# Attention on one Trainium2 core: ScalarE builds ten of sixteen mask rows, and TensorE's loop over the head pairs is written out

## What is computed

```python
seq = (x @ W_seq).reshape(N, H, DH)                 # N 2048, H 16, DH 32
scores = score1[:, :, None] + score2[:, None, :]    # s1 of row i plus s2 of column j, per head
scores = jax.nn.leaky_relu(scores, negative_slope=0.2)
scores = scores + (1.0 - adj)[None, :, :] * MASK_VAL
attn = jax.nn.softmax(scores, axis=-1)
hidden = jnp.einsum('hij,jhd->ihd', attn, seq).reshape(N, D_IN)
```

## Time and profile before

| What | Value |
|---|---|
| median of the runs | 1131.07 us |
| the profiled execution | 1135.76 us, its span 1133.9 us |
| first matmul of the attention | at 123.15 us |
| last reduction of the attention starts | at 562.38 us |
| mean granted TensorE clock | 0.964 |

### The profile page before, as it was taken

The page is one execution under the profiler, slowest core; times in us unless marked ns, Lnnn a source line. Parts: engine busy times, 40 slices in busy tenths (PEclk is TensorE's granted clock), DMA queues, the critical chain, the costliest instruction groups (busy, mean ns, idle before and its releaser), DMA issues. The chain is left out here.

```text
span 1133.9 us, 27344 instructions
## 1 busy us (share of the span) xinstructions
PE 1042.5 (92%) x11304; PEld 916.3 (81%) x11304; DVE 856.1 (75%) x1216; ACT 618.2 (55%) x939; POOL 315.0 (28%) x287
## 2 busy tenths in 40 slices
PE   5799687989898989978899999999999999999998
PEld 4576587989898989978867788888888887777887
DVE  4756999999999999997359953345876558985554
ACT  2226777777777777773045543334445445664432
POOL 1101434444444445463234200000026300005510
PEclk9899898999898989898989999999999999999999
DMA  8356011111111111153073510002016213444242
GB/s 299 112 192 240 20 58 40 40 40 40 40 46 52 40 40 40 40 168 113 2 285 123 174 58 1 1 1 75 1 48 212 85 42 126 131 130 150 75 141 101
DMA packets 51472, 102.68 MB, mean 91 GB/s; under 512 B 5889, under 2 KB 25985, under 8 KB 48770
## 3 DMA queue, kind: packets, MB, share of 16 engines
q1 hardware_dynamic: 44386, 81.68, 21.2%
q10 hardware_dynamic: 3888, 10.72, 2.6%
q0 software_dynamic: 3072, 8.39, 2.3%
HBM read 74.69 MB, written 26.08 MB: 89 GB/s over the span
## 5 line engine op out<-in xcount | busy, mean ns | idle before, releaser
L791 PE MATMUL bank<-arena 128*128 128x132 f16 x4096 | 298.0, 226 | 52.6 <-issue 43.3
L600 ACT ACTIVATE arena<-arena 128x1024 fp8e4<-128x1024 f32 x288 | 303.2, 1135 | 7.4 <-DMA arena<-s_rows 4.5
L791 PEld LDWEIGHTS bank<-arena 128*128 128x128 fp8e4 x4096 | 256.1, 100 | 56.8 <-issue 56.8
L653 DVE TENSOR_SCALAR arena<-arena 128x1024 uint8<-128x1024 f32 x224 | 205.9, 988 | 0.0
L1170 PE MATMUL bank<-xt,up_parts 128*128 128x512 f32 x768 | 186.3, 391 | 0.0
L1637 PE MATMUL bank<-down_parts,h_parts 128*128 128x512 f32 x768 | 184.5, 389 | 0.1
L795 PE MATMUL bank<-arena 128*128 128x66 f16 x4096 | 179.3, 199 | 0.0
L1637 PEld LDWEIGHTS bank<-down_parts,h_parts 128*128 128x128 f32 x768 | 144.0, 188 | 30.5 <-issue 0.5
L1170 PEld LDWEIGHTS bank<-xt,up_parts 128*128 128x128 f32 x768 | 142.3, 188 | 28.7 <-ACT relu_sb L1119 0.2
L795 PEld LDWEIGHTS bank<-arena 128*128 128x128 fp8e4 x4096 | 160.8, 100 | 0.0
L1144 DVE TENSOR_TENSOR relu_sb<-relu_sb 128x512 f32<-128x512 f32 x64 | 44.3, 692 | 116.9 <-ACT relu_sb L1119 111.7
(11 more groups left out here) (225 smaller groups left out, 1477.8 us busy)
## 6 DMA issues: line engine op xcount, KB each, us to landing
hid<-in_adjT SPq DMA_DIRECT2D x16, 1024.0 KB, 4.9
arena<-s_rows SPq DMA_DIRECT2D x30, 512.0 KB, 3.8
sorted_latent_rows<-zeros SPq DMA_DIRECT2D x1, 4992.0 KB, 18.7
xs<-sorted_latent_rows SPq DMA_DIRECT2D x39, 128.0 KB, 2.2
sorted_expert_rows<-expert_y SPq DMA_DIRECT2D x39, 128.0 KB, 1.7
arena<-in_x SPq DMA_DIRECT2D x4, 1024.0 KB, 12.0
xr<-in_x SPq DMA_DIRECT2D x16, 256.0 KB, 2.8
up_sb<-in_upT ACTq DMA_DIRECT2D x1, 4096.0 KB, 14.7
```

Source lines behind the costliest of these rows:

```text
L600: last = nc.scalar.activation(m8[:, k, j, :], s1b[:, k % 2, :], ACT.Sigmoid, bias=bias_now[:, k // 2, j:j + 1], scale=STEEP, saturate=False)
L653: last = nc.vector.tensor_scalar(mu8[:, k, j, :], s1b[:, k % 2, :], neg_s2[:, 2 * p + k // 2, j:j + 1], float(ONE8), ALU.is_gt, ALU.mult)
L791: last = nc.tensor.matmul(o, m8[:, k, j, i * P:(i + 1) * P], vs[:, b, j, :], start=(j == 0), stop=(j == T - 1))
```

## The change

VectorE's share of the rows goes from seven to six and ScalarE's from nine to ten. The hardware loop of TensorE becomes a Python loop: the same eight pairs of four units stand one behind the other in the program, with constant semaphore values. A semaphore increment (`pe_passed`), for which nobody waits, goes away. The other engines keep their loops.

```diff
-DVE_J = 7
+DVE_J = 6
...
-        act_passed, pe_passed = sem("act_passed"), sem("pe_passed")
+        act_passed = sem("act_passed")
...
-                with pe.Fori(0, PAIRS) as p:
+                for p in range(PAIRS):
                     for k in range(4):
                         b = k // 2
                         if k % 2 == 0:
                             pe.wait_ge(lo_ready, 2 * p + b + 1)
                         pe.wait_ge(sums_ready, 4 * p + k + 1)
                         pe.wait_ge(m_ready, 4 * p + k + 1)
-                        pe.sem_inc(pe_passed, 1)
                         for i in range(IT):
```

## The result

The changed kernel takes 1088.01 us (median of 4 runs, 1087.89 to 1089.21), the kernel before beside it 1132.41 us (4 runs). The ratio is 0.9615, with a 95% interval of 0.9595 to 0.9634. The forecast was 1086 us, in a range of 1078 to 1104. Of the two profiled executions, 1135.76 us became 1088.03, 47.7 us less.

A forecast was written before the change was run, and what follows sets the result against it. VectorE and TensorE were taken as both at their limit in the attention loop. 36.0 us up to the twenty-eighth collect and 9.1 behind it, together 45.1, took the median 1131.07 to 1086 us, range 1078 to 1104.

The forecast's parts named there:

- Two limits at once: Attention loop: VectorE (53.6 us per four units) and TensorE (52.9) both at their limit; one edit alone gains almost nothing.
- VectorE's two units, 24.24 us: VectorE's period in the loop after the change: 20.94 undisturbed, less 1.35 for compares, plus 4.65 disturbance.
- The masks cancelled: VectorE's L661 and L668: 256 words move from one mask to the other, 0.27 us each way, nothing in sum.
- The disturbance: Time VectorE loses to GpSimd per two units: taken as 4.65 us, with ends 4.65 and 5.84.
- the cheaper order of L661 and L737: Shared ports: VectorE's L661 stands ahead of GpSimd's L737 in every pair; if not, 1102 us, chance 0.20.
- The reading beside the fill: TensorE fetching straight code while the zero fill holds the DMA engines: 0 to 6 us, taken as 1.
- Its cover: ScalarE's wait of 5.81 us for the build absorbs its extra rows; about 1.2 us stays, cost 0.
- The ring that the slower rival supposed: ScalarE's wait before L608 is no slack but part of a cycle; 28.2 us per two units, 1141 us, chance 0.05.
- The start: Before the loop: VectorE's fewer compares and mask words bring the first collect 2.3 us sooner, to 153.1.
- The sum: Whole kernel: 36.0 us sooner at the twenty-eighth collect and 9.1 behind it, together 45.1 us.
- The clock rival: TensorE's clock falls at the remaining waits, one fall of 2.79 us per two units; 1107 us, chance 0.07.

The follow-up runs named there:

- rows_only: Kernel before with only the rows moved (VectorE six, ScalarE ten), TensorE's hardware loop kept: 1126.1 us, ratio 0.9921.
- unroll_only: Changed kernel with VectorE back at seven rows, so only TensorE's loop is written out: 1128.32 us, ratio 0.9965 to the kernel before.
- rows_7_6: Changed kernel with VectorE making seven rows in even units, six in odd ones: 1118.21 us, ratio 0.9870 to the kernel before.
- rows_6_7: Changed kernel with VectorE making six rows in even units, seven in odd ones: 1096.61 us, ratio 0.9679 to the kernel before.
- rows_6_5: Changed kernel with VectorE making six rows in even units, five in odd ones: 1079.04 us, ratio 0.9522 to the kernel before.
- fill_later: Kernel before with SyncE's zero fill issued after unit 28, behind the last jump of TensorE's loop: 1128.72 us, ratio 0.9963.
- half_jumps: Kernel before with VectorE at six rows and TensorE's loop as four passes of eight units, three jumps back: 1095.47 us, ratio 0.9672.
- rows_5: Changed kernel with VectorE at five rows and ScalarE at eleven in all units: 1088.24 us, ratio 0.9605 to the kernel before.

## Why the prediction was right

**Two limits at once.** This was the main step, and rows_only and unroll_only bear it out: 0.8% and 0.35% alone, 3.85% together.

**VectorE's two units, 24.24 us.** Measured 24.07. The row gave its 0.67 (six undisturbed compares take 4.06 us, seven 4.72). The masks cancelled: 1.76 and 2.82 us undisturbed, in sum as before. The disturbance was put at 4.65 and is 24.07 - 19.59 = 4.48. That the cheaper order of L661 and L737 becomes the regular one was argued from one pair of units before, and only two of that trace had it; it held in every pair, and rows_7_6 against rows_6_7 shows what the other order costs, 1.4 us per two units. The prediction named a rule of the Trainium skill in SBUF — State Buffer, section Who interferes with whom: whoever issues first holds the shared ports, and the other one blocks. The traces agree with both halves. In the changed kernel L737 ends 0.07 us behind L661, which was ahead of it. Before, L668 began 0.58 us behind L741 and lost 1.91 of the 2.05 us for which L741 still ran.

**TensorE.** The stops are gone, the clock is 1.00, and its wait is 0.82 us per two units (about 1 forecast). The reading beside the fill was put at 1 us; from the twenty-eighth collect to the last one it takes 513.57 - 476.82 = 36.75 us against 36.9. The stop for reading itself is only 0.20 us here. The traces of the other written-out kernels have stops of 0 to 2.1 us in all at this place, so 1 us is right in size and no better known than that.

**ScalarE.** Its cover was put at 1.2 us of idle time and is 1.77 to 1.82. The rows cost nothing. The ring that the slower rival supposed doesn't exist: in rows_6_5 ScalarE is busy 23.1 us of each 23.4, and the kernel gets faster.

**The start.** The first collect was forecast at 153.1 and stands at 151.20. This term was off by 1.9 us, and not through the edit. Counted from the first matmul of the attention, the rows give exactly what was forecast: the first collect comes 155.37 - 123.15 = 32.22 us behind it in the kernel before, 32.2 in unroll_only and fill_later too, which also have seven rows, and 151.20 - 121.29 = 29.91 in the changed kernel, 30.0 in rows_only and half_jumps with their six. That is 2.3 us. What varies is the start of the attention: in the twelve traces its first matmul stands between 120.9 and 123.8 us, without relation to the rows, and fill_later, which is the kernel before up to there, has it at 121.12 instead of 123.15. So the extra 1.9 us are chance; which part ahead of the attention varies is open.

**The sum.** 36.0 us forecast up to the twenty-eighth collect, 516.31 - 476.82 = 39.5 measured, of which 1.9 too much are the start and 1.6 the period (on average 24.12 us for two units); 9.1 behind it, measured 9.3; minus the 1.1 lost after the attention: 47.7 between the two profiled executions. By medians the gain is 44.4 us, 45.1 forecast. Without the 1.9 us of the start, which are chance, the terms of the traces sum to 45.8 us. That the 1.6 us of the period and the 1.1 us behind the attention nearly cancel is luck.

**The clock rival.** It did not come true: in the changed kernel the waits are 0.82 us and the granted clock is 1.00. But unroll_only shows that it was near. There waits of 2.0 us could be enough, not only those of 3.45; behind them the matmuls of two units are busy 24.8 us instead of 23.3. The length of the wait alone doesn't decide. In rows_7_6 the clock fell behind some waits of 2.9 us and stayed up behind others, as here (TensorE's timeline):

```profile
272.93 0.23 PE L791 MATMUL bank<-arena 128*128 128x132 f16 x1 [2.93 <-DVE arena L676]
...
273.51 1.09 PE L791 MATMUL bank<-arena 128*128 128x132 f16 x16
```

What decides between them is open. In the loops of all twelve traces no wait under 2.0 us was followed by a fall, apart from the second stops behind the jumps. So the prediction's conclusion held, but one reason it gave doesn't: that the matmul behind a wait takes 0.22 us says nothing of the clock. The one behind the first jump's stop takes 0.22 us too, the one at 250.23 in unroll_only 0.23, and in both places the clock falls shortly after. The section A second HAM failure mode: psum-queue depth-cycling in TensorE: Matmul & The Clock Gate (the Trainium skill) describes a clock that goes up and down behind short idle times. unroll_only agrees, at 0.94 for most of its units; the changed kernel, at 1.00, doesn't show it.

## What to carry to other kernels

When two engines run at nearly the same period, take each of them alone, with its stops, and write down both periods before costing an edit; here one edit alone brought under 1% and both together almost 4%. In this kernel TensorE's hardware loop pays at each jump back with two stops and a spell of the lower clock, some 7 us in all, and more if a large transfer runs then. Writing it out took all of that away, and passes of twice the length more than half. Where VectorE and GpSimd share ports, it counts who asks first: the place of one row ahead of a mask was worth 1.4 us per two units. And try the neighbours of a split: half a row further (rows_6_5) was another 9 us.

## What the runs showed of the hardware that was not expected

- A jump back goes with two instruction packets more (105, 97 and 91 with seven, three and no jumps), and behind it TensorE stops twice, about 3 and 0.3 to 1.8 us; with the DMA engines taken by the zero fill 5.82 and 3.69 us, without it 3.13 and 1.40.
- TensorE's clock fell behind waits of 2.0 us (unroll_only) and stayed up behind some of 2.93 us (rows_7_6).
- GpSimd's copy of 16 elements per partition, 0.68 us alone, takes 1.74 us if VectorE's mask is ahead of it, and so delays all that follows on GpSimd.
- In rows_5 the full ScalarE didn't show as idle time of VectorE, but, if the reading above is right, as longer compares (6.49 us for five), since GpSimd's late L741 then fell on them. A full engine may hide in another's durations.
